# Gated delta rule scan in a macaron block: batch 1 two steps behind batch 0, w in another column quarter, two more products a step

## What is computed

```
def step(S, inp):
    qi, ki, ui, wi = inp
    attn = jnp.tril(qi @ ki.transpose(0, 1, 3, 2))
    u_i = ui - wi @ S
    o_i = qi @ S + attn @ u_i
    return (S + ki.transpose(0, 1, 3, 2) @ u_i, o_i)
```

## Time and profile before

| what | us |
|---|---|
| median of three runs | 570.79 |
| lowest and highest of the three | 568.96, 572.97 |
| the profiled execution, its own time | 564.4 |
| its span in the profile | 562.6 |

### The profile page before, as it was taken

How to read it: one execution, slowest core, us unless ns; L and a number is a source line. 1 busy time by engine, 2 the same in 40 slices (tenths; PEclk the granted TensorE clock), 3 DMA queues, 4 the chain that set the end, 5 groups by cost and what they waited for, 6 DMA issues and landing times. The chain is left out here.

```text
span 562.6 us, 12845 instructions
## 1 busy us (share of the span) xinstructions
PE 406.0 (72%) x5009; PEld 319.8 (57%) x5010; DVE 319.2 (57%) x819; ACT 225.3 (40%) x453; POOL 142.4 (25%) x154
## 2 busy tenths in 40 slices
PE   0776599925985668889999988977996370059990
PEld 0664399913545557767787666753454360059980
DVE  4550465436968498777455556455488846026533
ACT  1233055614556367877342000174566221015550
POOL 4427135520006792000000000020222202714441
PEclk9999899976899759999899999986998555569996
DMA  9963401130000000000000000047000082141005
GB/s 190 279 197 91 121 21 38 33 93 2 0 0 1 3 3 4 5 5 3 2 3 1 1 1 1 1 92 152 1 1 0 0 269 81 52 118 36 33 28 164
DMA packets 32709, 29.92 MB, mean 53 GB/s; under 512 B 6800, under 2 KB 25776, under 8 KB 32656
## 3 DMA queue, kind: packets, MB, share of 16 engines
q1 hardware_dynamic: 23760, 20.96, 13.3%
q10 hardware_dynamic: 6400, 3.08, 3.3%
q0 software_dynamic: 2496, 5.13, 2.8%
HBM read 16.54 MB, written 9.21 MB: 46 GB/s over the span
## 5 line engine op out<-in xcount | busy, mean ns | idle before, releaser
L303 ACT ACTIVATE hT<-bank,b1s 128x128 f32<-128x128 f32 x184 | 52.4, 370 | 92.2 <-PE bank L260 91.3
L206 POOL DMA_INDIRECT ysort<-Y,row x46 | 44.8, 974 | 71.3 <-DVE Y L382 65.2
L260 PE MATMUL bank<-xT,w1s 128*128 (+1 forms) x368 | 51.0, 283 | 3.5 <-DVE xT L405 3.5
L276 PE MATMUL bank<-W,hT 128*128 x368 | 50.4, 280 | 3.1 <-ACT hT L303 2.9
L260 PEld LDWEIGHTS bank<-xT,w1s 128*128 128x128 f32 x368 | 46.6, 198 | 4.7 <-DVE xT L405 4.1
L276 PEld LDWEIGHTS bank<-W,hT 128*128 128x128 f32 x368 | 44.6, 191 | 5.3 <-issue 4.8
L1382 POOL TENSOR_TENSOR m_DSQ<-DEL 128x512 f32<-128x512 f32 x4 | 4.1, 1041 | 159.2 <-POOLq L767 156.5
L1054 DVE TENSOR_TENSOR d_BD<-bank,quarter 128x2048 f32<-128x2048 f32 x16 | 36.5, 2288 | 13.5 <-PE bank L760 13.5
L199 POOL DMA_INDIRECT xsort<-xr,pos x32 | 31.4, 980 | 48.4 <-DVE pos L361 39.3
L964 ACT ACTIVATE d_BD<-d_TP 32x512 f32<-32x512 f32 x64 | 40.5, 633 | 0.9
L248 PE MATMUL bank<-ident,xs 128*128 128x128 f32 x46 | 8.3, 318 | 29.3 <-DMA xs<-xsort 29.3
(11 more groups left out here) (297 smaller groups left out, 928.7 us busy)
## 6 DMA issues: line engine op xcount, KB each, us to landing
W<-in_L_ffn_w SPq DMA_DIRECT2D x2, 2048.0 KB, 12.7
xsort<-pad ACTq DMA_DIRECT2D x2, 1483.5 KB, 20.4
xs<-xsort SPq DMA_DIRECT2D x10, 258.0 KB, 4.0
G<-ysort SPq DMA_DIRECT2D x8, 256.0 KB, 4.0
b2bc<-in_L_ffn_b SPq DMA_DIRECT2D x2, 512.0 KB, 19.6
m_pairs<-FS SPq DMA_DIRECT2D x4, 256.0 KB, 5.0
m_pairs<-firT SPq DMA_DIRECT2D x4, 256.0 KB, 4.9
m_pairs<-VP SPq DMA_DIRECT2D x4, 256.0 KB, 5.1
```

The source lines that it names most:

```text
L206: gp.indirect_dma_start(ysort, bass.IndirectOffsetOnAxis(row[:, t:t + 1], 0), Y[:, t, :], None).then_inc(y_stored, 16)
L260: mm = pe.matmul(pH[s % 2][:, j * P:(j + 1) * P], w1s[:, s, j * P:(j + 1) * P], xT[:, bass.ds(t, 1), :], start=True, stop=True)
L276: mm = pe.matmul(pY[s % 2][:, 0:D], hT[:, s % 2, j, :], W2[:, bass.ds(e, 1), j, :], start=(j == 0), stop=(j == FC - 1))
L303: act.activation(hT[:, s % 2, j, :], pH[s % 2][:, j * P:(j + 1) * P], ACT.Gelu, bias=b1s[:, s, j:j + 1]).then_inc(h_ready, 1)
```

## The change

The two batches get semaphores of their own. Batch 1 runs LAG = 2 steps behind batch 0, so that the loop has 34 passes: in the first two only batch 0 works, in the last two only batch 1. `w_state` writes one quarter further (c + 1), and `subtract` reads from there. In passes 1 to 31 of the loop, two products of the identity with the block mask (128 x 128) are run, into columns of banks 2 and 0 that nobody reads: one between q and the state additions, one after the additions, ahead of `turn_fl`. `v_stats` stays after passes 7, 15, 23 and 31 of the loop.

```diff
-        ws_psum = sem("ws_psum")
-        u_ready = sem("u_ready")
-        s_psum, s_ready = sem("s_psum"), sem("s_ready")
+        ws_psum, u_ready, s_psum, s_ready = ([sem(f"{n}{b}") for b in range(B)] for n in ("ws_psum", "u_ready", "s_psum", "s_ready"))
...
+        LAG = 2
+
+        def w_rows(b, n):
+
+            c = (n + 1) % CT
+            return slice(c * C, (c + 1) * C)
+
+        def active(b, n):
+
+            return 0 <= n - b * LAG < STEPS_S
...
                     if n > 0:
-                        pe.wait_ge(s_ready, n * B + b - B + 1)
-                    pe.matmul(banks[b][c * C:(c + 1) * C, 0:P], WT[:, cols], SB[:, b, :], start=True, stop=True).then_inc(ws_psum, 1)
+                        pe.wait_ge(s_ready[b], n)
+                    pe.matmul(banks[b][w_rows(b, n), 0:P], WT[:, cols], SB[:, b, :], start=True, stop=True).then_inc(ws_psum[b], 1)
...
+                def keep_warm(bank, start):
+
+                    pe.matmul(banks[bank][:, P:2 * P], cst["ident"][:], cst["blk"][:], start=start, stop=True, skip_group_check=True)
+
...
-                    pe.wait_ge(u_ready, n * B + b + 1)
+                    pe.wait_ge(u_ready[b], n + 1)
...
-                for n in range(STEPS_S):
-                    w_state(0, n)
-                    w_state(1, n)
+                for n in range(STEPS_S + LAG):
+                    both = [b for b in range(B) if active(b, n)]
+                    for b in both:
+                        w_state(b, n - b * LAG)
                     if n == STEPS_S // 2:
 
                         pe.wait_ge(fl_taken, NG)
-                    q_state(0, n)
-                    q_state(1, n)
-                    add_state(0, n)
-                    add_state(1, n)
+                    for b in both:
+                        q_state(b, n - b * LAG)
+                    if 0 < n < STEPS_S:
+                        keep_warm(2, False)
+                    for b in both:
+                        add_state(b, n - b * LAG)
+                    if 0 < n < STEPS_S:
+                        keep_warm(0, True)
                     if 2 * n < NT:
                         turn_fl(2 * n)
                         turn_fl(2 * n + 1)
...
-                    ve.wait_ge(ws_psum, n * B + b + 1)
-                    ve.tensor_tensor(U[rows, tile, :], U[rows, tile, :], banks[b][rows, 0:P], ALU.subtract).then_inc(u_ready, 1)
+                    ve.wait_ge(ws_psum[b], n + 1)
+                    ve.tensor_tensor(U[rows, tile, :], U[rows, tile, :], banks[b][w_rows(b, n), 0:P], ALU.subtract).then_inc(u_ready[b], 1)
...
-                for n in range(STEPS_S):
-                    subtract(0, n)
-                    subtract(1, n)
-                    state(0, n)
-                    state(1, n)
-                    if n % 8 == 7:
+                for n in range(STEPS_S + LAG):
+                    both = [b for b in range(B) if active(b, n)]
+                    for b in both:
+                        subtract(b, n - b * LAG)
+                    for b in both:
+                        state(b, n - b * LAG)
+                    if n % 8 == 7 and n < STEPS_S:
```

More of the change, by code:

```diff
@@ L899, in add_state @@
                     rows, tile = slice(c * C, (c + 1) * C), b * TH + t
-                    pe.wait_ge(u_ready, n * B + b + 1)
+                    pe.wait_ge(u_ready[b], n + 1)
                     pe.matmul(banks[2 + b][:, 0:P], K[rows, tile, :], U[rows, tile, :], start=(n == 0),
-                              stop=(n == STEPS_S - 1), skip_group_check=True).then_inc(s_psum, 1)
+                              stop=(n == STEPS_S - 1), skip_group_check=True).then_inc(s_psum[b], 1)
                 def turn_fl(n):
@@ L926, in _ @@
                         turn_fl(2 * n + 1)
-                pe.wait_ge(u_ready, B * STEPS_S)
-                pe.wait_ge(s_ready, B * STEPS_S)
+                for b in range(B):
+                    pe.wait_ge(u_ready[b], STEPS_S)
+                    pe.wait_ge(s_ready[b], STEPS_S)
                 def intra(g):
@@ L1088, in subtract @@
                     rows = slice(c * C, (c + 1) * C)
-                    ve.wait_ge(ws_psum, n * B + b + 1)
-                    ve.tensor_tensor(U[rows, tile, :], U[rows, tile, :], banks[b][rows, 0:P], ALU.subtract).then_inc(u_ready, 1)
+                    ve.wait_ge(ws_psum[b], n + 1)
+                    ve.tensor_tensor(U[rows, tile, :], U[rows, tile, :], banks[b][w_rows(b, n), 0:P], ALU.subtract).then_inc(u_ready[b], 1)
                 def state(b, n):
-                    ve.wait_ge(s_psum, n * B + b + 1)
-                    ve.tensor_tensor(SB[:, b, :], banks[2 + b][:, 0:P], cst["blk"][:], ALU.mult).then_inc(s_ready, 1)
+                    ve.wait_ge(s_psum[b], n + 1)
+                    ve.tensor_tensor(SB[:, b, :], banks[2 + b][:, 0:P], cst["blk"][:], ALU.mult).then_inc(s_ready[b], 1)
                 def v_stats(c):
```

## The result

The changed kernel takes 601.39 us (median of four runs, 597.52 to 606.98) against 571.88 us; the ratio is 1.051, with an interval of 1.039 to 1.064. I had forecast no change that can be told, 573.9 us, with a range up to 582. The time lies outside it. Some runs of every kernel come out some per cent longer; the medians in this text include them, the ratios and their intervals leave them out.

A forecast was written before the change was run, and what follows sets the result against it. The scan was taken as bound by TensorE and VectorE taking turns, with TensorE's shape changes delaying additions. Step terms summed to a 65.7 us scan instead of 62.6, 3.1 us more, so 573.9 us, range 564 to 582.

The forecast's parts named there:

- Changes of shape: On TensorE, the next load starts 0.20 us after the last pass's start wherever the array piece changes shape.
- the whole ring: The chain of one plain step from w's load to the next w's load, 1.86 us in the kernel before.
- Quarters side by side: Both batches' w and q products overlap in four column quarters; last pass starts at 0.36 us instead of 0.79.
- serial rival: W and q stay serial in PE: 0.43 x 30 = 13 us more, 587 us; chance 0.09.
- A plain step of 1.84: A scan step without turns or statistics takes 1.84 us after the change instead of 1.86.
- the first, to which I had given 0.20 a step: Unused product between q and the additions: the first addition loads at 0.97 us rather than 0.77.
- the second, which I had hidden with a margin of 0.03: Unused product after the additions: w could load at 1.81 us, before batch 0's mask path at 1.84.
- The scan of 65.7 us at the full clock: Sum of all scan steps after the change, 65.7 us against 62.6 in the trace, with clock 1.00.
- The clock: Sign of a right forecast: TensorE's clock stays at 1.00 (2.4 GHz) in the scan.
- the rival with the clock: Earlier timed runs lose the clock in the scan and the unused products keep it: 567.5 us; chance 0.14.
- The rival of late additions: Additions don't overlap or second unused product is late: 0.17 us a step, 579 us; chance 0.14.
- Free unused products: Rival: the unused products ride along free, 30 steps x 0.19 = 5.8 us less, 568 us; chance 0.08.

The follow-up runs named there:

- held: The changed kernel with more unused products in light steps: three where one batch is alone, five after the statistics; 573.5 us, a single run.
- before_warm: The kernel before the change with the two unused products in each step and nothing else; 585.48 us, a single run.
- lag_four: The lag_only kernel with batch 1 four steps behind instead of two; 583.53 us, a single run.
- light_fill: The changed kernel without unused products in plain steps, with products in their neighbours' shape in the light steps alone; 587.4 us, ratio 1.036.
- burst: The changed kernel with twenty unused products ahead of the loop and two in step 0 as well; 602.75 us, a single run.
- held_again: The held kernel, no edit, now timed; median 589.38 us against 577.64 for the kernel before.
- lag_only: The changed kernel without unused products and with w back in its own quarter; 595.09 us (579.98 to 599.12).
- no_warm: The changed kernel without its two unused products; 591.89 us, ratio 1.038.

## Why the prediction was wrong

**Changes of shape: right.** 0.20 us from the start of the last pass to the next load, four times a step: in the held run q's last pass starts at 346.73 and the unused product loads at 346.93, its second pass starts at 347.15 and the addition loads at 347.35. before_warm met the whole ring, from w to w, within 0.02. The Trainium skill says so in words (TensorEngine Tiling, Key Properties): a change of tiling mode drains the engine. This trace agrees and gives 0.20.

**Quarters side by side: right.** W and q of both batches begin to load within 0.03 us at the low clock and 0.05 in the held run. The Trainium skill's rule that loads overlap running matmuls only where the row group differs (TensorE: Matmul & The Clock Gate, What overlaps and what doesn't), which goes with my serial rival, is not what this trace shows: all of these loads use every row.

**A plain step of 1.84: nearly.** At 2.4 GHz it is 1.93. Two terms were off. W of batch 1 loads with w of batch 0, not 0.21 later, since both masks are done when the second unused product ends; so the addition comes at 0.80 instead of 0.97. But the second subtraction starts 0.31 behind the first: they lie in different quarters of the partitions (lag_four). That puts batch 1's addition at 1.10, the second unused product at 1.51, and w at 1.93, while the first mask's path would have let it load at about 0.80 + 0.87 = 1.67. So the two unused products changed places in the account: the first, to which I had given 0.20 a step, costs 0.03 (0.80 instead of 0.77), and the second, which I had hidden with a margin of 0.03, costs some 0.26.

**The scan of 65.7 us at the full clock.** The held run has 70.3, with more products in the light steps than the changed kernel. The 21 plain steps account for 21 x 0.09 = 1.9 of the 4.6, turning steps (2.15 for 2.03, six of them) for 0.7; the remaining 2.0 lies almost all in the light steps, where it has its additional products. So at the full clock the change by itself would have been slower by something under 7.7 us.

**The clock: this is the step that failed.** The sum took the 1.00 of the earlier trace rows over to a schedule that has other waits and fewer separate passes. I had even set up the rival with the clock the wrong way round, as a gain, because the unused products use the whole array, and in the last lines allowed it 2 us behind the scan. What the runs showed in its place is 0.51, and it cost at least 26 us. That the products of the four quarters run at the same time is the saving, and as I read it that is also what takes work away from PE over time; no run measures this by itself. Shown: overlapped plain steps without fills lose the clock (light_fill, twice from a clock that had just come back); steps with both batches in one quarter keep it (lag_four in one execution, before_warm); the overlapped steps with unused products mostly keep it if they have it (held), can lose it even so (burst in the plain step behind the statistics, held_again among plain steps), and never got it back by themselves once low (changed kernel, burst). Not shown: what trips it in a given execution. Step 0 did in two kernels, and did not in lag_only and lag_four, where batch 0 is as much alone; there w and q share a quarter. Lag_only differs from no_warm in that alone, but one profiled execution of each can't show that this is the reason.

**The rival of late additions** was right in its mechanism, an unused product that ends later than the mask path, though not in its cause or size (0.09, not 0.17). Free unused products are refuted by before_warm.

## What to carry to other kernels

A step that saves PE time by running passes side by side can lose more than that through TensorE's clock: here 1.86 us became 1.65 at the full clock, and 2.19 at the low one (light_fill). When a change thins out PE's work, work out the time at both levels of the clock, and look for the lightest steps ahead of and in the loop. Work that is only there to keep the engine busy belongs in the shape of its neighbours, since each change of shape costs 0.20 us, twice per foreign product. And look for what can be moved out of the chain: the shorter plain step gave only 1.2 us of scan as long as statistics and turns stood in the steps, and 6.0 once they were out.

## What the runs showed of the hardware that was not expected

- In the changed kernel TensorE fell to 1.2 GHz although weight loads had paused for no longer than 1.18 us around it (298.51), and stayed there for the rest of the scan, in which its modelled busy time is 93.8 of 96.3 us. In held_again it fell with PE modelled busy for 3.40 of the 3.40 us before. A modelled busy share near one is no sign that the clock will hold or come back.
- Two of these subtractions in a row on the same quarter of partitions start 0.19 to 0.23 us apart on VectorE and overlap by some 0.06 (before, lag_four); on two different quarters the second starts 0.03 after the first has ended, 0.31 apart (held). It does not matter whether an operand comes from another quarter than the result: a subtraction takes about 0.28 either way (lag_only and held).
- At 1.2 GHz the change of shape costs 0.35 us from the last start instead of 0.20: in the changed kernel the last q pass starts at 342.25 (342.24 + 0.43 less one pass of 0.42), the next load at 342.60, and the other three changes of that step give 0.34 to 0.35.
